# Router and step-size terms on TensorE, GpSimd's passes spread, and sixteen batches written out, in a fused state-space and mixture-of-depths kernel

## What is computed

```python
x = x + s6(layernorm(x))                 # layer 1: a selective state-space scan
#   xp = h @ x_proj_w.T                  # 64 columns of rank, 16 of B, 16 of C
#   delta = softplus(d_rank @ dt_proj_w.T + dt_proj_b)
#   h_t = exp(delta * A) * h_(t-1) + delta * B_t * x_t      # 16 states a channel
#   y_t = sum over states(h_t * C_t) + x_t * D
x = x + ffn(layernorm(x))                # layer 2: routed attention and MLP
#   weights = layernorm(x) @ router_w + router_b            # one number a position
#   the 127 positions with the largest weights of a batch go through attention and a GELU MLP
```

## Time and profile before

| | |
|---|---|
| median of 3 runs | 4455.4 us (4452.94 to 4456.9) |
| profiled execution | 4463.26 us |
| its span | 4461.5 us |
| mean granted TensorE clock | 0.756 |
| PE, DVE, ACT, POOL busy | 69%, 84%, 64%, 75% of the span |
| first scan, last scan (L821) starts at | 79.96 us, about 3442 us |
| chain that ended last | mostly TensorE of the feed-forward stage |

### The profile page before, as it was taken

One profiled execution on the slowest core, in us unless ns is written; L12 is line 12 of the kernel. 1 busy time (PEld: TensorE's weight loads), 2 busy tenths in 40 slices (PEclk: granted clock), 3 DMA queues, 4 the chain that ended last, 5 costly groups with the idle time before them and its releaser, 6 DMA issues. The chain is left out here.

```text
span 4461.5 us, 61468 instructions
## 1 busy us (share of the span) xinstructions
PE 3066.8 (69%) x17574; PEld 1408.3 (32%) x17574; DVE 3768.9 (84%) x3027; ACT 2861.0 (64%) x4425; POOL 3363.5 (75%) x1716
## 2 busy tenths in 40 slices
PE   4667665766676666665665756666664289999997
PEld 1222232322232222222232323222222145555553
DVE  2999999999999999999999999999998754555552
ACT  5777777777778687868777777777774223332221
POOL 3999999999999999999999999999998100000010
PEclk7767676767766676667676767676775589999998
DMA  4454546463646455554545464636453300000000
GB/s 102 104 136 121 148 114 158 96 170 87 171 101 156 114 144 130 127 136 122 134 123 135 124 152 105 164 84 180 92 146 76 144 22 20 19 19 19 19 19 8
DMA packets 198219, 472.94 MB, mean 106 GB/s; under 512 B 60688, under 2 KB 61200, under 8 KB 197088
## 3 DMA queue, kind: packets, MB, share of 16 engines
q1 hardware_dynamic: 177136, 452.11, 40.3%
q0 software_dynamic: 20736, 16.88, 1.4%
HBM read 126.83 MB, written 73.43 MB: 45 GB/s over the span
## 5 line engine op out<-in xcount | busy, mean ns | idle before, releaser
L955 POOL TENSOR_TENSOR ch<-hid,cmat 128x1024 f32<-128x1024 f32 x1024 | 2385.4, 2358 | 92.7 <-DVE hid L821 76.4
L821 DVE TENSOR_TENSOR_SCAN hid<-place,inp 128x1024 f32<-128x1024 f32 x1024 | 2266.1, 2270 | 105.4 <-ACT place L671 87.3
L671 ACT ACTIVATE place<-delr,a_neg 128x1024 f32<-128x1024 f32 x1024 | 1126.8, 1111 | 293.6 <-DVE hid L821 190.2
L444 PE MATMUL ps_y<-ch,nsum 128*32 128x256 f32 x8192 | 856.5, 517 | 424.3 <-POOL ch L955 423.4
L810 DVE TENSOR_TENSOR inp<-place,bmat 128x1024 f32<-128x1024 f32 x816 | 941.6, 1211 | 64.2 <-ACT place L677 63.4
L455 PE MATMUL ps_y<-ident,ysb 128*128 128x128 f32 x1024 | 319.2, 408 | 599.0 <-ACT ysb L684 580.0
L444 PEld LDWEIGHTS ps_y<-ch,nsum 128*32 128x32 f32 x8192 | 254.6, 137 | 1025.6 <-POOL ch L955 753.2
L917 POOL TENSOR_TENSOR inp<-dxr,bmat 128x1024 f32<-128x1024 f32 x208 | 490.2, 2357 | 0.0
L455 PEld LDWEIGHTS ps_y<-ident,ysb 128*128 128x128 f32 x1024 | 230.5, 278 | 807.9 <-ACT ysb L684 759.1
L1216 POOL DMA_INDIRECT out_rows<-row,idx_out x16 | 41.1, 2571 | 532.3 <-issue 298.4
L439 PE MATMUL ps_y<-xhT,dskip 128*32 128x256 f32 x2048 | 260.8, 600 | 134.2 <-ACT xr L691 134.2
(11 more groups left out here) (176 smaller groups left out, 4202.8 us busy)
## 6 DMA issues: line engine op xcount, KB each, us to landing
dxr<-dxT SPq DMA_DIRECT2D x1024, 128.0 KB, 2.4
delr<-delT SPq DMA_DIRECT2D x1024, 128.0 KB, 2.4
xr<-in_x SPq DMA_DIRECT2D x32, 1024.0 KB, 6.6
bmat<-b_and_c SPq DMA_DIRECT2D x256, 128.0 KB, 3.4
cmat<-b_and_c SPq DMA_DIRECT2D x256, 128.0 KB, 3.1
x_rows<-xr SPq DMA_DIRECT2D x16, 2048.0 KB, 7.7
out_rows<-xr SPq DMA_DIRECT2D x32, 1024.0 KB, 5.1
w<-in_w SPq DMA_DIRECT2D x2, 4096.0 KB, 24.4
```

Source lines behind the costliest of these rows:

```text
L444: last = pe.matmul(ps_y[q * CH:(q + 1) * CH, 0:2 * P], nsum[:], ch[:, g, q * 2 * P:(q + 1) * 2 * P], start=False, stop=(g == GROUPS - 1))
L671: nc.scalar.activation(place[:, PLACE[par, c, g], :], delr[:, c % 2, :], ACT.Exp, scale=a_neg[:, i:i + 1])\
L821: nc.vector.tensor_tensor_scan(hid[:, g, :], place[:, PLACE[par, c, g], :], inp[:, g, :], 0.0, ALU.mult, ALU.add).then_inc(hid_ready, 1)
L955: nc.gpsimd.tensor_tensor(ch[:, g, :], hid[:, g, :], cmat[:, g, :], ALU.mult).then_inc(ch_ready, 1)
```

## The change

Six things change in `scan_phase`.

1. The router sum of VectorE is gone, with the copy of `rw` into `aux` and the tile `junk`. It is split in two: the part of the first layer's normalised x comes from the projection, whose weights are widened from 96 to 128 columns with 32 copies of `router_w`, so `xpT` rows 96 to 127 hold it, and eight one-column products turn it (`router_x`); the part of the scan's y comes from 32 products of `ysb` with four columns of `rw_chunk` each (`router_y`), for which `ysb` keeps all 16 chunks of a batch. ScalarE copies both, and GpSimd joins them with the sums and the two 1/sqrt in small passes of 8 columns.
2. The step-size terms of block 1 are added by TensorE, as those of blocks 2 and 3 were. The order in `aux` changes.
3. GpSimd's passes of block 0 are spread over chunks 13 and 14, and it makes its own input in 12 chunks, not 13. The softplus of block 2 moves by one chunk, into the batch that it belongs to.
4. The statistics of both layer norms are laid over more places, and `MAKE_OUT` begins one place later.
5. GpSimd's product goes in place: `hid` x `cmat` overwrites `hid`, `ch` is gone, and a scan waits until TensorE has summed the tile that its buffer held.
6. The loop over batches is gone: all 16 are written out on each engine.

```diff
-SUMS1 = {(5, 3): range(0, 3), (6, 0): range(3, 6), (6, 1): range(6, 9), (6, 2): range(9, 13), (6, 3): range(13, 17)}
-SUMS2 = {(0, 2): range(0, 2), (0, 3): range(2, 4), (1, 0): range(4, 6), (1, 1): range(6, 8), (1, 2): range(8, 10),
-         (1, 3): range(10, 12), (2, 0): range(12, 13), (2, 1): range(13, 15), (2, 2): range(15, 17)}
-MAKE_OUT = ((3, 1), (3, 2), (3, 2), (3, 3), (3, 3), (4, 0), (4, 0), (4, 1))
+SUMS1 = {(5, 0): range(0, 1), (5, 1): range(1, 2), (5, 2): range(2, 3), (5, 3): range(3, 5), (6, 0): range(5, 7),
+         (6, 1): range(7, 10), (6, 2): range(10, 13), (6, 3): range(13, 17)}
+SUMS2 = {(0, 2): range(0, 2), (0, 3): range(2, 3), (1, 0): range(3, 4), (1, 1): range(4, 5), (1, 2): range(5, 6),
+         (1, 3): range(6, 9), (2, 0): range(9, 11), (2, 1): range(11, 13), (2, 2): range(13, 15), (2, 3): range(15, 17)}
+MAKE_OUT = ((3, 2), (3, 2), (3, 3), (3, 3), (4, 0), (4, 0), (4, 1), (4, 1))
-Z = (12, 13, 15)
+Z = (12, 13, 16)
-DELTA = {(13, 0): (1, 0, 0), (13, 1): (1, 0, 1), (13, 2): (1, 0, 2), (13, 3): (1, 0, 3),
-         (14, 3): (1, 1, 0), (15, 0): (1, 1, 1), (15, 2): (1, 1, 2), (1, 0): (0, 1, 3),
-         (2, 3): (0, 2, 3), (7, 3): (0, 3, 3)}
+DELTA = {(13, 0): (1, 0, 0), (13, 2): (1, 0, 1), (14, 0): (1, 0, 2), (14, 1): (1, 0, 3), (0, 1): (0, 1, 3),
+         (4, 1): (0, 2, 3), (7, 3): (0, 3, 3)}
-ADD_TERMS = {(2, 0): ((0, 2), (0, 3), (1, 1)), (2, 1): ((1, 1), (1, 2), (2, 1)),
+ADD_TERMS = {(1, 0): ((14, 3), (14, 3), (15, 1)), (1, 1): ((15, 1), (15, 1), (15, 3)),
+             (2, 0): ((2, 3), (2, 3), (3, 1)), (2, 1): ((3, 1), (3, 2), (4, 0)),
              (3, 0): ((5, 2), (5, 3), (6, 1)), (3, 1): ((6, 1), (6, 2), (7, 1))}
-       (0, 0): (0, 2, (0,)), (0, 1): (0, 2, (1,)), (0, 2): (0, 2, (2,)),
+       (1, 0): (0, 2, (0,)), (1, 1): (0, 2, (1,)), (1, 2): (0, 2, (2,)),
-RW_COPY = (2, 1)
-ROUTER = (2, 3)
+ROUTE_Y = {(0, 3): range(0, 5), (1, 1): range(5, 8), (1, 2): range(8, 10), (1, 3): range(10, 15), (2, 1): range(15, 16)}
+COPY_ROUTE_Y = (2, 3)
+ROUTE_X = (14, 1)
+COPY_ROUTE_X = (14, 3)
+SCALE_ROUTE_X = (15, 1)
+ROUTE_READ = {cs[0]: i + 1 for i, cs in enumerate(ROUTE_Y.values())}
-FINISH2 = (2, 3)
+FINISH2 = (3, 0)
-OWN_AT = tuple(range(1, 14))
+OWN_AT = (1, 2, 3, 5, 6, 7, 8, 9, 10, 11, 12, 15)
...
-        def batches(eng, body):
-
-            body(0, 0)
-            if nb_run > 2:
-                with eng.Fori(1, nb_run - 2, 2) as i:
-                    body(i, 1)
-                    body(i + 1, 0)
-            body(nb_run - 1, 1)
+        def batches(body):
+
+            for b in range(nb_run):
+                body(b, b % 2)
...
+            def router_x(b):
+
+                aux_free(b, ("route_x",))
+                for t in range(TC):
+                    last = pe.matmul(aux[:, t:t + 1], xpT[R + 2 * N:P, t * P:(t + 1) * P],
+                                     ident[R + 2 * N:P, R + 2 * N:R + 2 * N + 1], start=True, stop=True)
+                last.then_inc(aux_full, 1)
+
+            def router_y(b, cs, emptied):
+
+                if 0 in cs:
+                    pe.wait_ge(aux_emptied, emptied)
+                for c in cs:
+                    for t in range(2):
+                        last = pe.matmul(aux[:, 4 * t:4 * t + 4], ysb[:, c, t * P:(t + 1) * P], rw_chunk[:, c, :],
+                                         start=(c == 0 and t == 0), stop=(c == CHUNKS - 1 and t == 1))
+                last.then_inc(route_y_full, 1)
...
                     last = pe.matmul(ps_y[q * CH:(q + 1) * CH, 0:2 * P], nsum[:],
-                                     ch[:, g, q * 2 * P:(q + 1) * 2 * P],
+                                     hid[:, g, q * 2 * P:(q + 1) * 2 * P],
...
+            for cs in ROUTE_Y.values():
+                router_y(nb_run - 1, cs, nb_run * NUSE)
             pe.wait_ge(wcol_ready, nb_run)
...
+                if c in ROUTE_READ and has(b, 1):
+                    act.wait_ge(route_y_full, (b - 1) * len(ROUTE_Y) + ROUTE_READ[c])
+                nc.scalar.activation(ysb[:, c, :], ps_y[:, 0:2 * P], ACT.Copy).then_inc(ysb_ready, 1)
...
             copy_x1(last, 1, CHUNKS - 1)
-            copy_rw(last, nb_run * NUSE)
+            copy_router_y(last)
             ln2_sums(last, 1, range(17))
...
                 if has(b, 1) or c > 0:
-                    dve.wait_ge(ch_ready, tile(b, c, g) - GROUPS + 1)
+                    dve.wait_ge(ch_summed, tile(b, c, g) - GROUPS + 1)
...
-                        if has(b, 1) or c > 0:
-                            pool.wait_ge(ch_summed, tile(b, c, g) - GROUPS + 1)
-                        nc.gpsimd.tensor_tensor(ch[:, g, :], hid[:, g, :], cmat[:, g, :],
+                        nc.gpsimd.tensor_tensor(hid[:, g, :], hid[:, g, :], cmat[:, g, :],
```

220 lines of the change are left out of this document (140 added, 80 removed).

## The result

The change makes the kernel slower: 4518.5 us (median of 4 runs, 4511.7 to 4522.0) against 4455.9 us of the kernel before beside it, a ratio of 1.0139 [1.0124, 1.0154], 62 us where I had forecast 40 us less. The profiled execution took 4521.46 us, its span is 4519.7 us.

A forecast was written before the change was run, and what follows sets the result against it. VectorE was taken to bound the scan stage of about 3450 us; -72.5 of work + 21 idle + 1.5 prologue + 10 tail = -40 us, median 4455.4 to 4415 us, 8-in-10 range 4342 to 4480.

The forecast's parts named there:

- VectorE's own work: Scan stage: router sums go, one product more a batch; -72.5 us in all, all of it on the path.
- GpSimd in chunks 13 and 14: Its worst stretch: ends chunk 14 some 5 us behind, own input for chunk 15 0.4 us late; +0.4 us a batch.
- TensorE, chunks 14 to 0: Block 1's four-term sum, one half mostly slow, one mostly fast, delays next batch's scans: 1.7 us a batch, bounds 0 and 7.
- Rival (b): Half clock holds in chunks 14 to 0, VectorE waits 7 us a batch: +40 us, 4495 us, slower; chance 0.16.
- In-place product: Scans wait for TensorE's sums, not GpSimd's product; about 6 us are left, so nothing taken by itself.
- ScalarE, chunks 1 to 3: Softplus and statistics make it late by 1.4 + 1.5 us and one PE wait: 1.9 us idle, bounds 0 and 4.
- ScalarE, chunks 4 to 7: 42.5 us of work against 36.4: 4.0 us idle at scan 2 of chunks 5, 6 and 7, bounds 2.2 and 6.
- The written-out loop: Removes the "issue" stall at every second batch's first scan, 1.46 us, and a longer stall in chunk 1.
- Prologue +1.5 and tail +10: Prologue: extra constant, row sum, Newton step, +1.5 us; tail: ScalarE's copy waits 9.5 us for 64 router instructions, +10 us.
- (c): Rival: a half step of the half-clock case, ScalarE at upper bounds 4 and 6: +40, 4455 us, no change; chance 0.14.

The follow-up runs named there:

- a_block0: Changed kernel with GpSimd's four step-size passes of block 0 back in chunk 13: 4443.9 us, ratio 0.9956 to the kernel before.
- a_spread_first: Changed kernel with SyncE issuing three groups of `bmat` ahead of `dxr`, GpSimd untouched: 4477.4 us, ratio 1.0033 to the kernel before.
- b_inplace: Kernel before with only GpSimd's product written over `hid` and scans waiting for TensorE's sums: 4458.1 us, ratio 0.9994.
- a_short_route: Changed kernel computing only 10 of the 32 router products of `ysb`, the rest left out: 4457.2 us, ratio 0.9992 to the kernel before.
- a_copy_route: Changed kernel with ScalarE's copy of the router sum at (2, 2), not (2, 3): 4494.8 us, ratio 1.0087 to the kernel before.
- a_sums1: Changed kernel with the first norm's statistics back at their five old places: 4515.7 us, ratio 1.0136 to the kernel before.
- a_route_even: Changed kernel with the 16 chunks of router products over seven places, two or three in each: 4499.3 us, ratio 1.0089 to the kernel before.
- a_block0_short: Changed kernel with block 0's passes back in chunk 13 and only 10 of 32 router products computed: 4398.5 us, ratio 0.9880 to the kernel before.
- a_all3: Changed kernel with block 0's passes back in chunk 13, router products over seven places, their copy at (2, 2): 4441.8 us, ratio 0.9966 to the kernel before.
- a_best: Changed kernel: block 0 back, copy at (2, 2), products over seven places with four chunks at (1, 3), second statistics evened: 4480.8 us, ratio 1.0040 to before.
- b_unrolled: Kernel before with only its batch loop written out: 4440.0 us, ratio 0.9949.

## Why the prediction was wrong

The forecast was -40 us and the measurement +62. By its own terms:

- *VectorE's own work, -72.5.* Right in kind, 14 us too large: the stage has 58.9 us less busy time. The sums went as counted. But the added product cost 22.2 us, not 18.1 (963.8 against 941.6), and the scans 5.7 us more (2271.8 against 2266.1): four scans in a row take 8.98 us in chunk 1 above where they took 8.82; 0.05 us of that is a wait too short for the view. The overlap of one instruction with the next is lost behind a stall, and I had counted in pitches of undisturbed chunks. These two make 10 of the 14 us; the rest is not broken down.
- *GpSimd in chunks 13 and 14, +0.4 a batch.* The own input was late by 8.1 / 15 = 0.54 us, as worked out. The failed step is in the same paragraph: "it ends chunk 14 some 5 us behind". I asked there only who waits for the own input, and not who waits for the moved passes. SyncE does, for `dxr` of the next batch, and 16 `bmat` transfers stand behind it. That is 60.0 us, 4.0 a batch, a term that isn't in the sum at all. a_block0 takes it away (75 to 82 us, with what hangs on it) and a_spread_first takes it away without touching GpSimd (47). With the first the changed kernel is faster than before, though by 20 us and not by 40.
- *TensorE, chunks 14 to 0, 1.7 a batch (0 to 7).* In that stretch VectorE waits 0.4 us in all for TensorE's sums, and no decay is late there. I took one half sum mostly slow and one mostly fast; in batch 6 they take 4.8 and 3.7 us. Rival (b), whose sign came true, did not happen by its mechanism: the granted clock is 1.00 from 1573.00 to 1581.60, where the products wait for `bmat`, and no scan there waits for TensorE. Late decays in chunks 15 and 0 do come with the passes back in chunk 13 (a_block0), 1.25 us a batch. Two thirds of that stand at scan 2 of chunk 15 behind `router_x`, whose eight products and copy my forecast put at nothing; the rest was not looked into.
- *In-place product, 0.* Right: b_inplace is the same as before, and the whole change has 0.4 us of waits for sums.
- *ScalarE, chunks 1 to 3, idle 1.9 (0 to 4).* Too low: 5.55 us on average (2.15 + 1.66 + 0.30 + 1.77 = 5.9 in batch 6), above my upper bound; 3.65 us more in each of 15 batches is 55 us. The kernel before had 4.2 us there, so I forecast a gain and got a loss. I had added ScalarE's own durations and one wait. What is missing is TensorE's order, the second failed step: 20 router instructions of 4.43 us between the sums and `ysb`. I had written that it "delays `ysb` of chunk 0 by up to 2 us, which is inside the 1.9"; ScalarE waits 4.28 us there and 3.5 on average. a_short_route, 65 us faster with a third of the products, shows the size of the term. The other half of the sentence, "in (1,3) ScalarE comes later anyway", was right: the products of (1, 3) take 4.41 us and end at 1400.70, and `ysb` of chunk 1 starts at 1400.96 without a wait for them, as in all 15 batches:

```profile
1400.96 0.36 ACT L745 ACTIVATE ysb<-ps_y 128x256 f32<-128x256 f32 x1
```

- *ScalarE, chunks 4 to 7, idle 4.0.* The size is right, about 4.5, at scan 2 of chunks 4, 6 and 7 and not of 5, 6 and 7. A part of the cause is another: some 1.9 us of it (27.9 / 15) is the late copy of the router sum ahead of the four-term sum, gone in a_copy_route. a_sums1 shows that the new places of the statistics in chunks 5 and 6, part of my reckoning, cost nothing. That the size fits is partly luck.
- *The written-out loop.* Counted inside the idle time; alone it is worth 23 us, more than the 1.46 us of every second batch.
- *Prologue +1.5 and tail +10.* The first scan is 2.5 us later, the tail 6 us longer. ScalarE waits in it for 64 router instructions, 13.65 us at the half clock all through, my upper bound of 13.7, not the 9.5 I took; the rest of the tail is shorter than I had it.

```profile
3502.88 13.65 PE L446 MATMUL aux<-rw_chunk,ysb 128*128 128x4 f32 x64
```

(TensorE's timeline in the tail, and ScalarE's below.)

```profile
3516.63 0.18 ACT L647 ACTIVATE route_y<-aux 128x8 f32<-128x8 f32 x1 [13.12 <-PE aux L446]
```

The stage by measured terms: -58.9 us of work, +108.4 us of idle time, of which 60 are the `bmat` wait. Idle time that the forecast had put at 8.0 us a batch is about 15 (224.2 / 15), where the same count gives 7.7 before.

One sum of the rivals is wrong in itself: (c) puts ScalarE at 4 and 6 in place of 1.9 and 4.0, which is 4.1 us a batch or +62 us, and adds only +40.

The gains of the single edits don't add up. Taken from a_block0, the router's shortening gives 34 us; taken from the kernel after, 65. Nor do a_route_even and a_copy_route add. VectorE's idle time in us by chunk, summed over batches 1 to 15 from its timeline in the profiled executions (in these kernels chunks 8 to 14 have none), shows why:

| kernel | 0 | 1 | 2 | 3 | 4 | 5, 6 | 7 | 15 |
|---|---|---|---|---|---|---|---|---|
| before | 8.0 | 58.8 | 3.8 | 0.0 | 0.0 | 0.0 | 31.1 | 0.4 |
| after | 0.0 | 20.9 | 55.9 | 6.5 | 27.9 | 8.3 | 29.1 | 63.7 |
| a_block0 | 6.3 | 3.5 | 50.2 | 3.2 | 26.4 | 10.0 | 26.2 | 13.6 |
| a_short_route | 0.0 | 1.5 | 27.2 | 0.0 | 27.6 | 11.9 | 27.0 | 62.8 |
| a_block0_short | 5.4 | 0.0 | 23.4 | 0.0 | 26.5 | 10.2 | 25.4 | 15.7 |
| a_copy_route | 0.0 | 20.6 | 55.8 | 8.0 | 0.4 | 7.0 | 35.8 | 62.7 |
| a_all3 | 10.3 | 0.0 | 24.2 | 53.0 | 0.0 | 10.1 | 31.5 | 16.9 |

The stall of chunk 1 needs both causes, the late product of GpSimd and the long row of router products behind it: either edit takes it away, 17 or 19 us, and the second one then finds 3.5 us left. That is the larger part of the 24 us by which the two ledger gains differ (56.4 and 32.7).

What stays open: the stall of 1.8 us at scan 2 of chunk 2 stands in every version with the router on TensorE but a_best, and I didn't settle what makes it. A stall in chunk 7 stands in every kernel here, the one before too.

## What to carry to other kernels

When a step is moved, follow each semaphore that it raises to the engine that waits, and then read what stands behind that wait in the same queue: here the loss was in transfers that needed nothing from the moved pass, and one reordering gave 47 us back. Work given to an engine that is idle a third of the time isn't free when it lands between two steps of a chain; count it at its slow duration and at the place where it stands, not over the batch. And when several edits share one engine's order, try them in pairs, since two gains of 22 us gave nothing together.

## What the runs showed of the hardware

- The router products ran at the half clock in the tail, although the profile shows TensorE busy all through. Windows of the kernel after, in the tail and at the start of chunk 2 of batch 6 (columns as in the earlier trace rows):

```profile
3502.90:3516.50 13.60, 13.60 (x65) 13.55 (x64) 0.00 (x0) 0.39 (x1) 0.00 (x0) 0.50 0.44 155
...
1392.50:1394.30 1.80, 1.80 (x20) 1.70 (x20) 0.94 (x1) 1.80 (x3) 1.80 (x2) 0.88 0.00 0
1394.60:1395.90 1.30, 1.30 (x16) 1.13 (x16) 1.05 (x1) 1.30 (x4) 0.70 (x2) 1.00 0.00 0
1396.20:1400.80 4.60, 4.50 (x24) 4.33 (x20) 2.83 (x2) 4.54 (x11) 4.23 (x2) 0.51 0.53 118
```

  The 64 instructions of the tail take 0.213 us each at 0.50. In chunk 2 TensorE had done 16 sums of 128x256 and the first of 12 router instructions when the clock rose (0.88 in the first of these windows); at 1.00 eight router instructions take 1.05 us, 0.13 each; then the clock is back at 0.50 in the next 20, with no gap ahead of them. In a_best TensorE is busy 32.08 of 34.10 us at 0.50. In chunk 3 of the kernel after the clock rose once more during a four-term sum: its pairs of 128x512 take 2.04, 1.91, 1.91 and 1.23 us in a row, and the turn behind them 0.38 where the one behind the router products took 0.80. The Trainium skill ("TensorE: Matmul & The Clock Gate", LDWEIGHTS) has a load at its columns over 1.2 ns; by that estimate 128 columns are 107 ns. Both measured figures lie above that, by a quarter and by a factor of two: it was a low end, as the forecast had it.
- Sixteen transfers cost SyncE 7.46 us to issue, 0.47 us each, so a group of them behind a wait is late by the wait and by its own issuing.
- The six jumps back of a loop of seven iterations, which every engine runs, cost 23 us, just under 4 us each (b_unrolled). The Trainium skill ("Runtime: NRT & Kernel Launch", Instruction fetch mechanics) says that a taken branch outside the fetched pages forces a fetch and that straight code is prefetched; the trace agrees, no "issue" wait stands at a first scan in b_unrolled, and its size on VectorE before was 1.46 us.
